# Attention layer of a two-layer graph network fed from y by feature, the first norm carried as centred weights and scales

## The chip, the cores and the metric

The kernel runs on one core of one Trainium2 chip. The metric is the device time of one execution in microseconds (us); the lower the better. Three runs of the kernel before took 954.08, 954.56 and 954.85 us, median 954.56.

## What is computed

`x` is 128 batches x 128 nodes x 128 features, `adj` a 128x128 matrix. Cut to what matters here:

```python
h = relu(einsum('ts,bsh->bth', adj, x @ Wg0 + bg0))
h = relu(einsum('ts,bsh->bth', adj, h @ Wg1 + bg1))
for p in 1..4:                     # windows of p nodes
    last = lstm_last(Wih[p-1], Whh[p-1], ..., windows of p of h)
    h[last node of each window] = last
x1 = layernorm(x + h)              # no scale, no shift, over features
Xq, Xv = x1 @ W_lin.T, x1 @ W_val.T          # 4 heads of 32
e = sum_d leaky_relu(Xq[src] + Xq[dst]) * a + log(adj[src, dst] + eps)
attn = softmax of e over the edges of one src            # 256 edges
Y = sum over edges of attn * Xv[dst], by src
out = layernorm(x1 + Y @ W_out.T)
```

## The kernel before, in words

The program has two halves, `front` and `back`, each with a function for every engine; `program` runs first the one, then the other on each engine. Nothing schedules: every engine does its instructions in the order written, and semaphores tie them together. A **tile** is 4 batches (`BT`), 512 columns; there are 32.

`front` does the two graph products and the first LSTM pass (p = 1), then `for ph in phases[1:]` the passes p = 2, 3, 4. State is kept with features on the partitions, as a pair `hT_hi` + `hT_lo`, each 128 x (128 batches x 128 nodes). An LSTM item (one step t of one group of windows) is 9 or 12 TensorE (PE) products of 512 columns from the input (L431 to L433), for t > 0 another 12 from the state (L445, L446, L449), four gate functions on ScalarE (ACT, L537) and the tanh (L525), and on VectorE (DVE) the products L762, L765, L772, L779 and the cut into hi and lo (L750, L752). The last pass, p = 4, works on 8 groups of 16 batches, two at a time ("a pair"), four steps each; the groups 6 and 7 are its last pair, and their eight items end the LSTM.

`back` goes in slots. In slot n of `for n in range(FIRST, LAST)` (n = -3 to 46) each engine works on several tiles at once:

- GpSimd (POOL): `sum_halves(n + 3)` adds hi and lo of a tile into `hsum` (L919). `factors(n)` (L940 to L958) makes the scale `rstd` and the shift of the norms from the statistics, ten small instructions, for the first norm of tile n + 2 and the second norm of tile n - 2 - LAG.
- PE: `turn_h` (L978) transposes hsum. DVE adds the residual x (`residual`, L1178) into `y` and takes statistics (`stats_in`, L1185). ACT writes the normalized tile (`normalize_x1`, L1119, four instructions with scale and bias) into `x1_kept`. PE turns that back (`turn_x1`, L985), ACT copies it out (`x1_turned`, L1145, into `x1T`), and only then `project` (L993) multiplies it with the query and value weights.
- The queries are cut into hi and lo (`query_hi` ACT L1106, `query_lo` DVE L1190), `gather` (L1002, L1003) adds them over both ends of each edge, ACT takes the leaky relu (L1141), `edge_scores` (L1012) sums with `a`. The values are cut likewise (L1110, L1195).
- Eight tiles (`GT`) make a group of the softmax, spread over four slots on DVE (`softmax`, steps 0 to 7, two a slot; step 6 is one reciprocal of 256 columns, L1220).
- LAG = GT + 4 = 12 slots later the tile's values are gathered (`value_gather`, L1037, L1038), weighted (`weight_values`, DVE L1231), summed by source (`sum_by_source`, L1054), copied (L1137), multiplied with W_out (`output`, L1065), added to x1 (`add_mixed`, DVE L1237), normalized (`stats_out` L1243, `normalize_out` ACT L1131 and POOL L925), and stored by SyncE's queue (SP).

So slots 0 to 11 hold the first half of a tile's work alone, slots 12 to 31 both halves, slots 32 to 46 the second alone. The x tiles for the residual are loaded by SP in `run_sync`, 256 KB each, two ahead.

Of the kernel before, what the change touches and what calls it, by code (L numbers as in the profile page):

```python
# [12 lines left out]
P = 128  # L13
# [9 lines left out]
BT = 4  # L23


Part = namedtuple("Part", "S CREDIT phases sync gpsimd tensor scalar vector")

# [37 lines left out]
class Tables:  # L65


    def __init__(self, sb, HEADS, E):
# [13 lines left out]
        self.minus_half = sb("minus_half", [P, 2, BT])  # L82


def front(nc, sb, sem, tables, hT_hi, hT_lo, ident, adj_sb, psum, x, adj, Wg0, bg0, Wg1, bg1, Wih, Whh, bih, bhh,
# [56 lines left out]
    bias = sb("bias", [P, SKIPS * GATES])  # L142
# [33 lines left out]
             "row_edges onehots wT_psum wT_ready adj_psum adj_done eps_done log_done diag_done log_psum log_ready ends_ready sames shifted caps")  # L176
# [14 lines left out]
    def has(k):  # L191
        return 0 <= k < tiles

# [72 lines left out]
    def run_tensor(pe):  # L266
# [43 lines left out]
        def turn_back_weights():  # L310
            pe.wait_ge(raw_loaded[1], 48)
            pe.wait_ge(S["adj_done"], EC)
# [104 lines left out]
        for ph in phases[1:]:  # L417
            for it in range(ph.iters):
# [37 lines left out]
    def run_scalar(act):  # L456
# [63 lines left out]
        for ph in phases[1:]:  # L520
            for it in range(ph.iters):
# [31 lines left out]
    def run_vector(dve):  # L553
# [66 lines left out]
        def ends_and_sames():  # L620
# [6 lines left out]
            dve.tensor_tensor(same_b[:, 0:E - 1], sorted_row[:, 0, 1:E], sorted_row[:, 0, 0:E - 1], ALU.is_equal).then_inc(S["sames"], 1)  # L627

# [92 lines left out]
        for n in range(SLOTS):  # L721
# [3 lines left out]
            elif n == 2:  # L725
                ends_and_sames()
                adjacent()
            elif n == 3:
# [9 lines left out]
        for ph in phases[1:]:  # L738
            for it in range(ph.iters):
# [15 lines left out]
                for tile, t, k, forgets in ph.body():  # L755
# [3 lines left out]
                    c = cell[s][:, 0:ph.width]  # L759
                    if t > 0:  # L760
# [30 lines left out]
def back(nc, sb, sem, tables, before, hT_hi, hT_lo, ident, psum, x, a, src, out):  # L791
# [5 lines left out]
    B = x.shape[0]  # L797
    tiles = B // BT
# [6 lines left out]
    LAG = GT + 4  # L805
    RING = LAG + 6
    X_RING = 2
    FIRST, LAST = -3, tiles + LAG + 3
# [6 lines left out]
    x1T = sb("x1T", [P, 2, TW])  # L815
# [3 lines left out]
    rows, row_a, row_b, exps = (sb(n, [P, E]) for n in ("rows", "row_a", "row_b", "exps"))  # L819
    attn = sb("attn", [P, 2, EC, P])  # L820
    x_res = sb("x_res", [P, X_RING, BT, P])
    hsum = sb("hsum", [P, 2, TW])
    y = sb("y", [P, 2, BT, P])
# [3 lines left out]
    rstd = sb("rstd", [P, 2, 2, BT])  # L827
    shift = sb("shift", [P, 2, 2, BT])
# [513 lines left out]
```

## Time and profile before

| | |
|---|---|
| median of 3 runs | 954.56 us |
| the profiled execution, its own time | 952.53 us |
| its span | 950.7 us |
| PE busy | 891.7 us (94%) |
| DVE busy | 680.2 us (72%) |
| ACT busy | 628.5 us (66%) |
| POOL busy | 207.8 us (22%) |
| last LSTM product on PE starts | 628.91 us |
| granted TensorE clock, mean | 0.988 |

Times inside the trace count from the start of the span. PE's matmul rows overlap each other, so the pace of a group is read from the starts of its neighbours, not from the length of one. A float32 product of 128 columns is two rows of the trace. The profiled execution's own time is 1.8 us above its span, and the median of the runs 2.0 us above that.

### The profile page before, as it was taken

Reading aid. Unit: us, or ns where it says so; the run is one execution under the profiler, and the core shown is the slowest. Engines: PE = TensorE matmul, PEld = TensorE weight load, DVE = VectorE, ACT = ScalarE, POOL = GpSimd, SP = SyncE. Lnnn points to the kernel's source line nnn. Section 1 sums busy time; section 2 is a strip of 40 time slices with the busy share of each in tenths; the row PEclk is TensorE's granted clock in tenths of the full one; section 3 lists DMA queues with packets and bytes.
Section 4 is the critical chain, followed back from the end, with each engine's and each line's share of the span. In section 5 each row is a group of like instructions: output and inputs, shape, how many; then the busy total and the mean of one; then the engine's idle time right before and its main releaser. Section 6 shows DMA issues by size and latency. Waiting matters only on the chain.

```text
span 950.7 us, 15626 instructions
## 1 busy us (share of the span) xinstructions
PE 891.7 (94%) x5523; PEld 771.9 (81%) x5523; DVE 680.2 (72%) x1365; ACT 628.5 (66%) x1170; POOL 207.8 (22%) x568
## 2 busy tenths in 40 slices
PE   7999999989999999999999999958879999999895
PEld 6989988868777899999987878847657888888684
DVE  5777777777877777777777776754456786776764
ACT  2777777777777776767666666646766667666354
POOL 0000000000000000000001000026755666776665
PEclk9999999999999999999999999989999999999998
DMA  4212211000000000000000000001111122221112
GB/s 117 68 46 66 59 57 52 3 23 1 0 1 1 1 1 1 1 1 2 1 1 0 1 1 1 1 22 34 50 40 35 57 68 60 58 63 36 54 57 67
DMA packets 56700, 28.67 MB, mean 30 GB/s; under 512 B 2704, under 2 KB 56624, under 8 KB 56624
## 3 DMA queue, kind: packets, MB, share of 16 engines
q1 hardware_dynamic: 55248, 27.47, 10.3%
q8 instruction: 45, 0.74, 0.3%
q10 hardware_dynamic: 1376, 0.22, 0.1%
q14 instruction: 31, 0.25, 0.1%
HBM read 19.29 MB, written 8.39 MB: 29 GB/s over the span
## 4 chain that ended last, share of the span: by engine, by line
PE 78%; DVE 7%; ACT 7%; POOL 4%; issue 3%; DVEq 0%; POOLq 0%; ACTq 0%
PE psum L431 8%; PE psum L432 8%; PE psum L433 7%; PE psum L993 6%; PE psum L449 6%; PE psum L445 6%; PE psum L446 6%; PE psum L1054 4%; PE psum L349 3%; PE psum L367 3%; PE psum L377 3%; PE psum L1065 2%; ACT x_kept L1119 2%; PE psum L341 2%; PE psum L339 2%
## 5 line engine op out<-in xcount | busy, mean ns | idle before, releaser
L537 ACT ACTIVATE work<-psum,bias 128x512 f32<-128x512 f32 (+1 forms) x408 | 234.0, 622 | 30.5 <-PE psum L449 29.9
L919 POOL TENSOR_TENSOR hsum<-hT_hi,hT_lo 128x512 f32<-128x512 f32 x32 | 41.7, 1305 | 514.7 <-DVE hT_lo L752 514.7
L431 PE MATMUL psum<-hT_hi,w_hi 128*128 128x512 f32 (+1 forms) x408 | 148.0, 363 | 2.9 <-ACT work L537 2.2
L432 PE MATMUL psum<-hT_lo,w_hi 128*128 128x512 f32 (+1 forms) x408 | 147.8, 362 | 0.0
L433 PE MATMUL psum<-hT_hi,w_lo 128*128 128x512 f32 (+1 forms) x408 | 146.7, 359 | 0.0
L525 ACT ACTIVATE work<-work 128x512 f32<-128x512 f32 (+1 forms) x112 | 63.8, 569 | 102.9 <-DVE work L772 69.3
L445 PE MATMUL psum<-hs_hi,w_hi 128*128 128x512 f32 (+1 forms) x288 | 104.0, 361 | 2.0 <-DVE hs_hi L750 1.8
L779 DVE TENSOR_TENSOR work<-work 128x512 f32<-128x512 f32 (+1 forms) x112 | 68.5, 612 | 52.0 <-ACT work L525 52.0
L449 PE MATMUL psum<-hs_lo,w_hi 128*128 128x512 f32 (+1 forms) x288 | 104.2, 362 | 0.0
L446 PE MATMUL psum<-hs_hi,w_lo 128*128 128x512 f32 (+1 forms) x288 | 103.2, 358 | 0.0
L431 PEld LDWEIGHTS psum<-hT_hi,w_hi 128*128 128x128 f32 x408 | 76.8, 188 | 16.8 <-ACT work L537 5.3
L433 PEld LDWEIGHTS psum<-hT_hi,w_lo 128*128 128x128 f32 x408 | 76.9, 189 | 10.5
L432 PEld LDWEIGHTS psum<-hT_lo,w_hi 128*128 128x128 f32 x408 | 76.7, 188 | 9.7
L765 DVE TENSOR_TENSOR work<-work 128x512 f32<-128x512 f32 (+1 forms) x112 | 69.3, 619 | 20.8 <-ACT work L537 20.8
L480 ACT ACTIVATE work<-psum,bias 128x512 f32<-128x512 f32 x96 | 64.9, 682 | 26.2 <-PE psum L341 24.1
L993 PE MATMUL psum<-w_qv,x1T 128*128 128x128 f32 x512 | 66.4, 285 | 3.0 <-ACT x1T L1145 3.0
L993 PEld LDWEIGHTS psum<-w_qv,x1T 128*128 128x128 f32 x512 | 62.4, 199 | 5.9 <-ACT x1T L1145 5.9
L1231 DVE TENSOR_TENSOR va<-psum,attn 128x512 f32<-128x512 f32 x64 | 42.8, 682 | 32.2 <-PE psum L1038 32.1
L1054 PE MATMUL psum<-from_node,va 128*128 128x128 f32 x512 | 63.2, 277 | 2.0 <-DVE x_kept L1237 2.0
L1119 ACT ACTIVATE x_kept<-y,shift,rstd 128x128 f32<-128x128 f32 x128 | 52.7, 482 | 16.0 <-POOL shift L958 16.0
L445 PEld LDWEIGHTS psum<-hs_hi,w_hi 128*128 128x128 f32 x288 | 54.1, 188 | 11.3 <-DVE hs_hi L750 4.6
L449 PEld LDWEIGHTS psum<-hs_lo,w_hi 128*128 128x128 f32 x288 | 54.1, 188 | 10.6 <-DVE hs_lo L752 4.1
(186 smaller groups left out, 1910.5 us busy)
## 6 DMA issues: line engine op xcount, KB each, us to landing
work<-x SPq DMA_DIRECT2D x32, 256.0 KB, 2.9
x_res<-x SPq DMA_DIRECT2D x32, 256.0 KB, 2.8
out<-x_kept SPq DMA_DIRECT2D x32, 256.0 KB, 2.3
work<-L_gnn_Wih SPq DMA_DIRECT2D x4, 256.0 KB, 3.1
work<-L_gnn_Whh SPq DMA_DIRECT2D x3, 256.0 KB, 2.8
bg_all<-L_gnn_bg ACTq DMA_DIRECT2D x2, 64.0 KB, 5.1
edge_row_i<-L_gnn_src SPq DMA_DIRECT2D x1, 128.0 KB, 5.6
adj_sb<-adj SPq DMA_DIRECT2D x1, 64.0 KB, 3.1
```

Of the source, the lines that this page charges most:

```text
L431: pe.matmul(out, w_hi[:, w, g, :], xh, start=True, stop=False)
L432: pe.matmul(out, w_hi[:, w, g, :], xl, start=False, stop=False)
L433: mm = pe.matmul(out, w_lo[:, w, g, :], xh, start=False, stop=(t == 0))
L445: pe.matmul(out, w_hi[:, w, g, :], hh, start=False, stop=False)
L446: pe.matmul(out, w_lo[:, w, g, :], hh, start=False, stop=False)
L449: pe.matmul(out, w_hi[:, w, g, :], hl, start=False, stop=True).then_inc(gate_psum[g], 1)
L537: op = act.activation(gate[s][g][:, 0:ph.width], psum[:, 4 * s + g, 0:ph.width], ACT.Tanh if g == G else ACT.Sigmoid, bias=bias[:, b:b + 1])
L765: op = dve.tensor_tensor(i_g, gate[s][I][:, 0:ph.width], gate[s][G][:, 0:ph.width], ALU.mult)
L779: dve.tensor_tensor(h_full[s][:, 0:ph.width], gate[s][O][:, 0:ph.width], tanh_c[s][:, 0:ph.width], ALU.mult).then_inc(S["h_mul"], 1)
L993: mm = pe.matmul(psum[:, bank, b * P:(b + 1) * P], x1T[:, k % 2, b * P:(b + 1) * P], w, start=True, stop=True)
L1054: mm = pe.matmul(psum[:, sum_bank(k), b * P:(b + 1) * P], va[:, k % 2, c, b * P:(b + 1) * P], from_node[:, c, :], start=(c == 0), stop=(c ...
L1119: op = act.activation(x1_kept[:, k % RING, b, :], y[:, k % 2, b, :], ACT.Identity, bias=shift[:, at, 0, b:b + 1], scale=rstd[:, at, 0, b:b ...
```

## The change

What it does, part by part:

1. **y by feature.** The kernel gets one more input, x with the features first, 1 MB for each of 8 groups of 16 batches. SP loads it into `x_stage`. POOL issues, for each group j, a DMA that adds `hT_hi` into `hT_lo` in place (`sum_halves(j)`), and when that has landed one that adds `x_stage` in place (`add_x(j)`); after that `hT_lo` holds y = x + h with features on the partitions. Groups 0 to 5 are done in this way one after the other, with a wait for each landing, while the LSTM runs, and only then does POOL start with `factors`. Groups 6 and 7 are spread over slots 1, 3, 5, 7 and 9, each step after that slot's `factors`, with a wait for the landing of the step before.
2. **First norm as weights and scales.** The rows of W_lin and W_val have their mean taken off in `front` (`centre_back_weights`, four DVE instructions), so `project` can take y itself as it stands in `hT_lo`; the mean needs no subtracting. The scale `rstd` goes onto the queries as they leave PSUM (`query_hi` by DVE for tiles under LAG, in four ACT instructions after; `query_lo` as four DVE instructions), onto the attention weights (`edge_rstd`, `attention_out`, now on DVE, with two more small products on PE for each group of 8 tiles), and onto x1 in `add_mixed` (four DVE instructions in place of one). Gone are `sum_halves` on POOL's arithmetic, `residual`, `normalize_x1`, `turn_x1`, `x1_turned`, and three of the ten instructions of `factors` for the first norm. New is `read_turned` on ACT, a copy of the turned y.
3. **Entry into the last LSTM pair.** The turning, reading and statistics of tiles 0 and 1 and the queries of tile 0 stand among the items of the last pair on PE, ACT and DVE. The slots run from 0 to 47.
4. LAG is 13, `RING` 24, there are 8 store semaphores, and the softmax of a group goes over five slots with its reciprocal in two halves.

```diff
+        def centre_back_weights():
+            dve.wait_ge(raw_loaded[1], 48)
+            dve.wait_ge(S["adj_done"], EC)
+            for j in range(2):
+                dve.tensor_scalar(less[:, j * P:(j + 1) * P], w_raw[1][:, j, :], -1.0 / P, 0.0, ALU.mult, ALU.add,
+                                  accum_out=minus_mean[:, j:j + 1]).then_inc(S["w_means"], 1)
+            for j in range(2):
+                dve.wait_ge(S["w_means"], j + 1)
+                dve.tensor_scalar(w_raw[1][:, j, :], w_raw[1][:, j, :], minus_mean[:, j:j + 1], None, ALU.add).then_inc(S["w_centred"], 1)
...
                 for tile, t, k, forgets in ph.body():
+                    ending = in_last_pair(ph, it, k)
+                    if ending and t == 1:
+                        entry.turned(pe, k % 2)
                     from_input(tile, t, k)
+                    if ending and t == 0:
+                        entry.turn(pe, k % 2)
+                    if is_last(ph, it, k):
+                        pe.wait_ge(S["gates_read"], ph.items_after - 1 + CREDIT)
+                        entry.query(pe)
                     if t > 0:
                         from_state(k, forgets)
...
+                    if in_last_pair(ph, it, k) and t == 0:
+                        entry.read(act, s)
...
+                    if in_last_pair(ph, it, k):
+                        if t == 1:
+                            entry.stats(dve, s)
+                        elif is_last(ph, it, k):
+                            entry.scale_query(dve)
...
-    LAG = GT + 4
-    RING = LAG + 6
-    X_RING = 2
-    FIRST, LAST = -3, tiles + LAG + 3
+    LAG = GT + 5
+    RING = LAG + 11
+    GROUP = before.phases[-1].batches // BT
+    LAST = tiles + LAG + 3
...
+        for j in range(tiles // GROUP):
+            if j:
+                sp.wait_ge(S["y_made"], 16 * j)
+            sp.dma_start(x_stage[:, :].bitcast(F32), xt[j]).then_inc(S["x_staged"], 16)
...
-            pool.tensor_tensor(hsum[:, k % 2], hT_hi[:, cols].bitcast(F32), hT_lo[:, cols].bitcast(F32), ALU.add).then_inc(S["hsum_ready"], 1)
+        def sum_halves(j):
+            cols = slice(j * GROUP * TW, (j + 1) * GROUP * TW)
+            pool.wait_ge(FS["tiles_done"], last_pass.tiles_before + j + 1 + before.CREDIT)
+            pool.dma_start(y_by_feature[:, cols], hT_hi[:, cols].bitcast(F32), accum_op=ALU.add).then_inc(S["h_summed"], 16)
+
+        def add_x(j):
+            cols = slice(j * GROUP * TW, (j + 1) * GROUP * TW)
+            pool.wait_ge(S["h_summed"], 16 * (j + 1))
+            pool.wait_ge(S["x_staged"], 16 * (j + 1))
+            pool.dma_start(y_by_feature[:, cols], x_stage[:, :].bitcast(F32), accum_op=ALU.add).then_inc(S["y_made"], 16)
...
+        sums = tiles // GROUP
+        for j in range(sums - 2):
+            sum_halves(j)
+            add_x(j)
+            pool.wait_ge(S["y_made"], 16 * (j + 1))
+        factors(-2)
+        factors(-1)
+        for n in range(LAST):
             if has(n - 3 - LAG) and not late(n - 3 - LAG):
                 normalize_out(n, n - 3 - LAG)
-            if has(n + 3):
-                sum_halves(n + 3)
             if has(n + 2) or has(n - 2 - LAG):
                 factors(n)
+            for j in (sums - 2, sums - 1):
+                at = 1 + 4 * (j - sums + 2)
+                if n == at:
+                    sum_halves(j)
+                elif n == at + 2:
+                    add_x(j)
+                elif n == at + 4:
+                    pool.wait_ge(S["y_made"], 16 * (j + 1))
...
-            pe.wait_ge(S["xT_ready"], k + 1)
             if k:
                 pe.wait_ge(free, k)
             for b in range(BT):
-                mm = pe.matmul(psum[:, bank, b * P:(b + 1) * P], x1T[:, k % 2, b * P:(b + 1) * P], w, start=True, stop=True)
+                mm = pe.matmul(psum[:, bank, b * P:(b + 1) * P], y_of(k, b), w, start=True, stop=True)
...
+        def query_hi(k):
+            dve.wait_ge(S["factors_done"], k + 1)
+            dve.wait_ge(S["q_psum"], k + 1)
+            dve.tensor_tensor(xq_hi[:, :, :], by_bank(Q), rstd[:, k, 0, :].unsqueeze(2).broadcast_to([P, BT, P]), ALU.mult).then_inc(S["q_hi"], 1)
...
         def add_mixed(m):
             dve.wait_ge(S["o_psum"], m + 1)
-            dve.tensor_tensor(x1_kept[:, m % RING], by_bank(out_bank(m)), x1_kept[:, m % RING], ALU.add).then_inc(S["o_read"], 1)
+            for b in range(BT):
+                op = dve.scalar_tensor_tensor(out=x1_kept[:, m % RING, b, :], in0=x1_kept[:, m % RING, b, :], scalar=scale_of(m, b),
+                                              in1=psum[:, out_bank(m), b * P:(b + 1) * P], op0=ALU.mult, op1=ALU.add)
+            op.then_inc(S["o_read"], 1)
```

How the order of the instructions stands at three places. First PE at the end of the LSTM, before: the last products of the last item (L445, L446, L449), then turns of tiles 0 and 1 (L978, of hsum), the second turn of tile 0 (L985), and its queries and values (L993).

```order
L449 MATMUL psum<-hs_lo,w_hi 128x512
L978 MATMUL psum<-ident,hsum 128x128 [waits f_onehots,f_a_loaded,f_ends_ready,b_hsum_ready,f_wT_ready,f_gates_read]
L978 MATMUL psum<-ident,hsum 128x128 [waits b_y_done,b_hsum_ready]
L985 MATMUL psum<-ident,x_kept 128x128 [waits b_x1_done,b_y_done]
L993 MATMUL psum<-w_qv,x1T 128x128 [waits b_xT_ready]
L993 MATMUL psum<-w_qv,x1T 128x128 x3
```

Now the same place in the change: L443 to L445 are the input products of the last item, L1058 the queries (first) and the values of tile 0, L1051 a turn of y, L1075 and L1076 the gather.

```order
L445 MATMUL psum<-hT_hi,w_lo 128x512
L1058 MATMUL psum<-w_qv,hT_lo 128x128 [waits f_wT_ready,f_gates_read]
L1058 MATMUL psum<-w_qv,hT_lo 128x128 x3
L457 MATMUL psum<-hs_hi,w_hi 128x512 [waits f_h_hi]
L458 MATMUL psum<-hs_hi,w_lo 128x512
...
L461 MATMUL psum<-hs_lo,w_hi 128x512
L1058 MATMUL psum<-w_qv,hT_lo 128x128 [waits f_a_loaded,f_onehots,f_ends_ready]
L1058 MATMUL psum<-w_qv,hT_lo 128x128 x3
L1051 MATMUL psum<-ident,hT_lo 128x128 [waits b_y_done,b_y_made]
L1051 MATMUL psum<-ident,hT_lo 128x128 x3
L1075 MATMUL psum<-ends,xq_hi 128x256 [waits f_gates_read,b_xq_ready]
```

The queries of tile 0 have moved in front of the last item's state products, the second turn is gone, and what follows the LSTM's last product is the values of tile 0, a turn, and the gather.

Second, DVE around the last LSTM item in the change (L801 to L818 are the item's products, L784 and L786 its cut): L1269 and L1279 scale the queries of tile 0, L1286 cuts its values, L1263 takes statistics of tile 2.

```order
L1269 TENSOR_TENSOR xq_hi<-psum,rstd 128x512 [waits b_q_psum,b_factors_done]
L1279 SCALAR_TENSOR_TENSOR xq_lo<-psum,rstd,xq_hi 128x128 [waits b_q_hi]
L1279 SCALAR_TENSOR_TENSOR xq_lo<-psum,rstd,xq_hi 128x128 x3
L801 TENSOR_TENSOR work<-work 128x512 [waits f_f_ready]
L804 TENSOR_TENSOR work<-work 128x512 [waits f_ig_ready]
L811 TENSOR_TENSOR work<-work 128x512 [waits f_ig_done,f_fc_done]
...
L786 TENSOR_TENSOR hT_lo<-work,hT_hi 128x128x4 [waits f_h_hi]
L1286 TENSOR_TENSOR hT_lo<-psum,hT_hi 128x512 [waits b_v_hi,f_caps,f_log_ready]
L1263 BN_STATS stats<-x_kept 128x6 [waits b_factors_done,b_y_done]
```

In the kernel before the item's first product (L762) followed the item before it directly; now the scaling of the queries, which waits for POOL's `factors_done`, stands between them.

Third, POOL in the change: the last two adding DMAs of the part ahead of the slots and the first factors (L995 to L1009, seven instructions), and further on, after the factors of slot 1, the sum for group 6.

```order
L970 DMA hT_lo<-hT_hi 128x2048
L976 DMA hT_lo<-x_stage 128x2048
L995 TENSOR_TENSOR diff<-stats 128x4
L998 TENSOR_TENSOR m_sum<-stats 128x4
L1000 TENSOR_SCALAR half_diff<-diff 128x4
L1003 TENSOR_SCALAR m_eps<-m_sum 128x4
L1005 TENSOR_TENSOR diff_sq<-half_diff 128x4
L1007 TENSOR_TENSOR var_eps<-m_eps,diff_sq 128x4
L1009 TENSOR_TENSOR rstd<-var_eps,minus_half 128x4
...
L970 DMA hT_lo<-hT_hi 128x2048
```

No `factors` stand on POOL before the twelve adding DMAs of groups 0 to 5.

## Rows read from the trace of the kernel before

**Rows 1.** Stages: us, busy PE, PEld, DVE, ACT, POOL (x), clock, DMA share, GB/s.
```profile
634.00:642.00 8.00, 1.92 (x8) 1.28 (x8) 2.76 (x10) 2.15 (x5) 5.83 (x20) 0.56 0.22 66
642.00:707.00 65.00, 53.25 (x424) 43.90 (x424) 32.80 (x76) 46.79 (x98) 42.33 (x113) 0.98 0.14 41
725.00:875.00 150.00, 148.18 (x1225) 130.88 (x1226) 109.10 (x259) 103.40 (x218) 100.08 (x239) 1.00 0.20 57
```

**Rows 2.** Chain of waits (start, us, what): starts of slots 1, 4, 5, 13.
```profile
649.25 2.07 PE psum L993 x16
...
666.32 2.06 PE psum L993 x16
...
669.00 1.55 ACT x_kept L1119 x4
...
672.01 2.06 PE psum L993 x16
...
725.08 2.05 PE psum L993 x16
```

**Rows 3.** PE timeline (start, us, line, count): the LSTM's last product.
```profile
628.91 0.39 PE L449 MATMUL psum<-hs_lo,w_hi 128*128 128x512 f32 x1
```

**Rows 4.** DVE timeline: group 4 cut; last item's first product; its cut.
```profile
593.56 0.69 DVE L752 TENSOR_TENSOR hT_lo<-work,hT_hi 128x512 fp32r<-128x512 f32 x1
...
628.00 0.69 DVE L762 TENSOR_TENSOR work<-work 128x512 f32<-128x512 f32 x1 [1.35 <-ACT work L537]
...
633.03 0.69 DVE L752 TENSOR_TENSOR hT_lo<-work,hT_hi 128x512 fp32r<-128x512 f32 x1
```

**Rows 5.** PE timeline, a slot with both halves, until the next one.
```profile
807.43 1.05 PE L1065 MATMUL psum<-w_outT,yT 128*128 128x128 f32 x8
808.32 1.95 PE L993 MATMUL psum<-w_qv,x1T 128*128 128x128 f32 x16
810.10 1.95 PE L1054 MATMUL psum<-from_node,va 128*128 128x128 f32 x16
811.98 0.64 PE L1012 MATMUL psum<-leaky,a_wide 128*32 128x256 f32 x8
812.55 0.50 PE L1037 MATMUL psum<-hT_hi,to_r 128*128 128x512 f32 x1
...
813.13 0.64 PE L978 MATMUL psum<-ident,hsum 128*128 128x128 f32 x4
...
814.71 0.62 PE L985 MATMUL psum<-ident,x_kept 128*128 128x128 f32 x4
815.09 0.36 PE L1002 MATMUL psum<-ends,xq_hi 128*128 128x256 f32 x1
...
816.54 1.95 PE L993 MATMUL psum<-w_qv,x1T 128*128 128x128 f32 x16
```

**Rows 6.** DVE timeline of that slot: four statistics, and the instruction after.
```profile
809.24 0.87 DVE L1243 BATCH_NORM_STATS2 stats<-x_kept 128x6 f32<-128x128 f32 x4
810.04 0.69 DVE L1190 TENSOR_TENSOR xq_lo<-psum,xq_hi 128x512 fp32r<-128x512 f32 x1
```

**Rows 7.** POOL timeline: first and last of the ten of `factors`.
```profile
635.31 0.20 POOL L940 TENSOR_TENSOR diff<-stats 128x4 f32<-128x4 f32 x1 [115.05 <-DVE stats L1185]
...
638.35 0.20 POOL L958 TENSOR_TENSOR shift<-minus_mean,rstd 128x4 f32<-128x4 f32 x1
```

**Rows 8.** Chain of waits: slot 32's first sum, one turn of the late slots.
```profile
883.76 2.02 PE psum L1054 x16
...
923.56 1.17 PE psum L1065 x8
...
931.87 1.17 PE psum L1065 x8
```

**Rows 9.** DMA queue of SP (packets, MB, share of 16 engines' span).
```profile
q1 hardware_dynamic: 55248, 27.47, 10.3%
```

**Rows 10.** DMA issues: x tiles (KB each, us from issue to landing).
```profile
x_res<-x SPq DMA_DIRECT2D x32, 256.0 KB, 2.8
```

More of the change, by code:

```diff
@@ L26 @@
 Part = namedtuple("Part", "S CREDIT phases sync gpsimd tensor scalar vector")
+Entry = namedtuple("Entry", "turn turned query read stats scale_query")
 class LstmPhase:
@@ L1080, in slot @@
             if has(n + 2):
-                turn_h(n + 2)
+                turn(n + 2)
             if has(n):
@@ L1246, in slot @@
         def slot(n):
+            if n > 0 and n % GT == LAG % GT and has(n - LAG):
+                attention_out((n - LAG) // GT)
             if has(n - 2 - LAG):
@@ L1250, in slot @@
             if has(n):
-                query_lo(n)
+                if n:
+                    scaled_query(n)
                 value_lo(n)
-            g, quarter = softmax_at(n)
-            if g is not None:
-                softmax(g, 2 * quarter)
+            g, part = softmax_at(n)
+            for step in STEPS[part][0] if part is not None else ():
+                softmax(g, step)
             if has(n - LAG):
@@ L1258, in slot, with enter_stats, enter_scale_query, run_vector @@
             if has(n + 2):
-                residual(n + 2)
-                stats_in(n, n + 2)
+                stats_in(n + 2)
             if has(n - LAG):
                 weight_values(n - LAG, 1)
-            if g is not None:
-                softmax(g, 2 * quarter + 1)
+            for step in STEPS[part][1] if part is not None else ():
+                softmax(g, step)
+        return stats_in, scaled_query, slot
+    def enter_stats(dve, k):
+        stats_in, _, _ = vector_steps(dve)
+        stats_in(k)
+    def enter_scale_query(dve):
+        _, scaled_query, _ = vector_steps(dve)
+        scaled_query(0)
+    def run_vector(dve):
+        _, _, slot = vector_steps(dve)
         dve.wait_ge(FS["log_ready"], 1)
         dve.wait_ge(FS["caps"], 2)
-        for n in range(FIRST, LAST):
+        for n in range(LAST):
             slot(n)
-    return Part(S, 0, None, run_sync, run_gpsimd, run_tensor, run_scalar, run_vector)
-def program(nc, x, adj, Wg0, bg0, Wg1, bg1, Wih, Whh, bih, bhh, W_lin, W_val, a, W_out, src, dst, out):
+    entry = Entry(enter_turn, enter_turned, enter_query, enter_read, enter_stats, enter_scale_query)
+    return Part(S, 0, None, run_sync, run_gpsimd, run_tensor, run_scalar, run_vector), entry
+def program(nc, x, xt, adj, Wg0, bg0, Wg1, bg1, Wih, Whh, bih, bhh, W_lin, W_val, a, W_out, src, dst, out):
     B = x.shape[0]
@@ L1301, in _ @@
                 second.sync(sp)
+            @block.tensor
+            def _(pe):
+                first.tensor(pe, entry)
+                second.tensor(pe)
+            @block.scalar
+            def _(act):
+                first.scalar(act, entry)
+                second.scalar(act)
+            @block.vector
+            def _(dve):
+                first.vector(dve, entry)
+                second.vector(dve)
             @block.gpsimd
```

288 lines of the change are left out of this document (152 added, 136 removed).

## The prediction

> **What bounds the kernel now.** I read the busy times by stage first, then the chain of waits, then one slot of each stage on the engines that meet there. The stages differ. While the LSTM runs, PE has no gap; its last product starts at 628.91 [rows 3], so it ends about 629.1. Then comes a hole: from 634 to 642 PE is busy 1.92 of 8 us and its granted clock is down to 0.56, half of full speed [rows 1]: the first tile goes through addition, statistics, factors, normalization and a second turn before a projection can start, and slot 1 starts only at 649.25 [rows 2]. In the early slots PE is busy 53 of 65 us [rows 1] but the chain runs through ACT: projection, the cut of the values, four normalizing instructions (1.55 us), the second turn, its copy, next projection. A slot takes 672.01 - 666.32 = 5.69 us [rows 2]. Slots 1 to 12 take 725.08 - 649.25 = 75.8 us, 7.5 above twelve times 5.69; those are the slots in which DVE's softmax and the first gathers begin. In the slots with both halves PE is full (148.2 of 150 us [rows 1]) and one takes 816.54 - 808.32 = 8.22 us [rows 5]. The late slots hang on a loop (output, add, statistics, factors, normalization, copy, output) that covers two slots in 931.87 - 923.56 = 8.31 us [rows 8].
>
> **The sum**, along the path, against the profiled execution (span 950.7).
>
> *Front.* Four DVE instructions of 128 columns and their waits; a DVE instruction of that size is spaced 0.2 us in rows 6, so about 1 us with the waits, and PE waits for `w_centred` before three transposes. PE has other work queued only behind them. I take +0.5, bounds 0 and 1.5.
>
> *Last pair.* PE is full, so what is put in counts whole. Turning y reads hT_lo with a step of four elements, as the turns of hsum do. Sixteen rows show 1.95 us and eight 1.05, so a row is (1.95 - 1.05)/8 = 0.112 apart from the next and the last one lasts 0.26; four strided turns show 0.64, so 0.12 to 0.127 each [rows 5]. I take 0.12; the four contiguous turns (0.62) leave it open that the step costs nothing. Eight turns and eight rows of queries: +1.9. ACT's two copies of a turned tile and DVE's statistics stand where PE has its t = 0 and t = 1 products queued; cover gone, the statistics alone would cost 1.6. So PE ends its last product at 631.5, DVE its last cut at 633.03 + 0.69 + 2.4 = 636.1 [rows 4].
>
> *Entry.* DVE then cuts the values of tile 0 (0.7, as L1190 in rows 6), takes statistics (0.8, the spacing in rows 6), scales and cuts the queries of tile 1. Four DVE instructions of 128 columns that read PSUM have no row: from below four statistics, 0.80 [rows 6]; from above the four of ACT, 1.55 [rows 2]; I take 0.95, near the row of the same engine. So 636.1 + 0.7 + 0.8 + 0.8 + 0.95 = 639.3, and the gather of slot 1 starts there. On PE it lies 1.8 + 0.6 + 0.5 behind the slot's start, so slot 1 counts from 636.4 instead of 649.25. **-12.9.** Nothing is idle for long, so the clock should not fall to half.
>
> *Early slots.* ACT's normalization leaves the loop. What is late next is PE: 8.22 less the sum by source (811.98 - 810.10 = 1.88), output (0.89), two value gathers (0.58 each), the second turn (815.09 - 814.71 = 0.38), all from rows 5, is 3.93; with the projection now loading with a step of four, 16 rows at 0.12 instead of 0.112, +0.12: 4.05. DVE needs 0.7 + 0.95 + 0.7 + 0.8 = 3.15. POOL's ten instructions take 638.35 + 0.20 - 635.31 = 3.24 us [rows 7]; three of them go, one of which hung on a wait of its own, so 2.6. Factors made in slot n are used in slot n + 2 and end about 7.2 us after slot n starts; they are wanted at 9.2, 2 us later. Twelve slots: 48.6, and of the 7.5 us of softmax and first gathers I keep 5.5, since the reciprocal is halved but DVE now scales the queries too (bounds 0 and 12). Slot 13 starts at 636.4 + 54.1 = 690.5 instead of 725.08. **-21.7** more.
>
> *Slots with both halves.* Minus the second turn, plus the strided loads: 8.22 - 0.38 + 0.12 = 7.96. DVE has 109.1 of 150 us now, 6.0 a slot [rows 1]; it loses the residual (0.6) and gains twice 0.3, so it stays under 6.5. Before, 19 slots took 883.76 - 725.08 = 158.7 [rows 2, 8]. Now 158.7 - 19 x 0.26 = 153.8, less 1.9 for the sum by source that slot 13 has not yet (the lag is one more), plus 0.3 for the small products of each of three groups: 152.8. **-5.9.** Slot 32 at 843.3.
>
> *Late slots.* Before, 950.7 - 883.76 = 66.9. One slot more, 4.15, and in each of the 16 half of the 0.3 by which four instructions in `add_mixed` exceed one: +2.4. 73.5. **+6.6.** End at 916.8.
>
> *The adding DMAs.* No row shows one. Let D be the time from POOL's issue to the landing. From below: a copy. SP's queue moved 27.47 MB in 10.3% of 950.7 us of all engines [rows 9], 3.57 us a MB, so 3.7 for one transfer; a 256 KB load lands after 2.8 us [rows 10], 1.9 more than its own 0.9. That gives 5.6. An addition reads two operands: 1.9 + 7.4 = 9.3 if reads set the pace. I take **8**, between them, since rows of 8 KB replace packets of half a KB and SP's loads of x share the engines. From above I keep reads and writes each at half that speed, 1.9 + 14.8 = 16.7; nothing in the trace excludes it. Twice D matters. First, group 4 is cut at 594.2 [rows 4], then four additions and the first factors (2.7) must pass before DVE may scale the queries, wanted at about 629.1 (the last item's first DVE product is at 628.00 [rows 4]). The stall is 594.2 + 4D + 2.7 - 629.1 = 4D - 32.2, and it stands in front of the last LSTM item, whose products, cuts and all slots queue behind it. Second, the sum for group 6 is issued behind the factors of slot 1, at about 636.4 + 7.2 = 643.6. Each wait holds the factors behind it: four times D and another 2.6 must have passed when the factors of slot 10 are wanted in slot 12, at about 636.4 + 44.6 + 3.7 + 1.1 = 685.8. That stall is 4D - 39.6. At 8 both are nothing. POOL's issue costs about 1 us in a slack of 2.
>
> The Trainium skill, "Collectives: The Full Stack", in its section on why ReduceScatter is half of AllGather, says that an adding transfer runs at half the pace of a copy because it reads two sources; "DMA: Bandwidth & Descriptors", Anatomy of one DMA, gives 2.0 us plus the bytes by 436 GB/s for a copy. By these an addition would take an estimated 6.8 us and the sum would not change, since both stalls are nothing there too; the trace of before has no accumulating transfer to agree or disagree.
>
> *SP's queue*: the stores now stand behind all loads of x. The last load waits for group 6, in about slot 5; the first store is in slot 16. Nothing.
>
> Sum: 950.7 - 12.9 (the 2.4 of front and last pair are in it) - 21.7 - 5.9 + 6.6 = 916.8 span, 918.6 as that execution's own time (952.53 against 950.7), 2.0 more for the median (954.56): **920.6**.
>
> **Rivals.**
> *A, as summed*, 909 to 932 by the bounds of the softmax extra (-5.5, +6.5), the reads, and the four-piece instructions. Chance 0.52.
> *B, additions a little slow*, D from 9 to 13. At 11: 11.8 + 4.4 = 16.2 more, 937. For it: two reads already give 9.3. Against it: that row is of small packets. 0.17.
> *C, another engine's order binds the slots.* DVE has 15 instructions a slot in fixed order, each waiting for PE, ACT or POOL; if the early slots take 5 us instead of 4.05 (+11) and the full slots stay at 8.22 (+5), 936. For it: before, early slots were bound by exactly such a chain with PE at 82%. Against it: the four-instruction link is gone and every remaining one has slack. 0.18.
> *D, slower than before: the additions hold the LSTM's last item.* At D = 16.7 the stalls are 34.6 and 27.2, 982. It decides from 8D - 71.8 = 34, D = 13.2. In front of the last pair only 35 us are free, and POOL does nothing else for it. Chance 0.11.
> *E*, that y is not there in time for other reasons and the gain is eaten to no change: 0.02.
> That the change does not do what it says: the second turn and the normalization are gone from the order, so the gain in PE's products is certain; only its cover can fail, which is C.
>
> A measurement of this kernel tells about 0.2% from no change. Faster A, B and C, 0.87; same 0.02; slower 0.11. The range takes A, C and most of B: 906 to 948; what it leaves out is D, the end of B, and a gain beyond 48 us.
>
> **What would show it.** Right: PE without a gap over 1 us between the last LSTM product and slot 2, clock at 1.00; early slots of 4.0 to 4.3 us; projection rows 0.12 apart; full slots at 8.0; late loop 8.6 for two slots; landing of the additions at 8 us. Wrong: DVE idle before the scaling of tile 0's queries with POOL as releaser (B, D); DVE idle in slots 4 to 10 on POOL's `rstd`; early slots of 5 us with PE waiting for DVE's query cut (C).

## The result, and the profile after

| | before | after |
|---|---|---|
| median | 954.7 us (954.08 to 954.91, 4 runs) | 974.12 us (973.65 to 975.92, 4 runs) |
| span of the profiled execution | 950.7 us | 972.1 us |
| PE busy | 891.7 us (94%) | 933.5 us (96%) |

The change makes the kernel slower, by about 2%: the ratio of the times is 1.0208, 95% interval 1.019 to 1.0226, clear of no change. The forecast was 920.6 us and a range of 906 to 948. PE has 112 matmul rows fewer (5411 against 5523) and is busy 42 us longer.

The page of the kernel after, its groups of instructions for the projection, and the queue of the adding transfers (packets, MB, share):

```profile
L1058 PE MATMUL psum<-w_qv,hT_lo 128*128 128x128 f32 x512 | 124.9, 397 | 1.0 <-DVE hT_lo L1286 1.0
L1058 PEld LDWEIGHTS psum<-w_qv,hT_lo 128*128 128x128 f32 x512 | 122.1, 328 | 1.3 <-DVE hT_lo L1286 1.2
...
q0 software_dynamic: 2304, 16.78, 8.5%
```

The same groups of the kernel before, by shape, with both kinds of turn:

```profile
L993 PEld LDWEIGHTS psum<-w_qv,x1T 128*128 128x128 f32 x512 | 62.4, 199 | 5.9 <-ACT x1T L1145 5.9
L978 PEld LDWEIGHTS psum<-ident,hsum 128*128 128x128 f32 x128 | 19.4, 207 | 11.0 <-issue 8.3 <-ACT work L537 1.2
L985 PEld LDWEIGHTS psum<-ident,x_kept 128*128 128x128 f32 x128 | 13.8, 143 | 25.7 <-DVE y L1178 20.2 <-issue 5.3
```

Here is the answer. The stationary operand is the one that PE loads ahead of a product (the rows PEld), the moving operand the one that then streams through. The projection's 512 loads of a stationary operand took 199 ns each and take 328; the time in which PE is loading for it goes from 62.4 to 122.1 us. The turns show that it was to be seen: a load with a step of four (L978) took 207 ns, one of neighbouring columns (L985) 143, but the spacing of the turns hardly showed it [rows 5].

The chain of waits of the kernel after: the projections that start slots 2, 3 and 4, then slots 13 and 14, then 16 and 17, then the sum that starts slot 32.

```profile
644.45 3.73 PE psum L1058 x16
650.37 3.73 PE psum L1058 x16
656.28 3.73 PE psum L1058 x16
...
711.44 3.81 PE psum L1058 x16
718.59 3.73 PE psum L1058 x16
...
737.97 3.73 PE psum L1058 x16
747.65 3.73 PE psum L1058 x16
...
896.65 2.02 PE psum L1131 x16
```

Sixteen rows take 3.73 us, 0.233 apart, where before they were 0.112 apart [rows 5]. An early slot takes 5.91 us (5.69 before [rows 2]), a full one 9.68 (8.22 before [rows 5]).

Stages of the kernel after (same columns as [rows 1]): at the entry PE is idle for 1.0 us of 8 where it had been idle for 6.1 [rows 1], its clock does not fall, and in the full slots DVE, ACT and POOL have less to do per microsecond than before.

```profile
634.00:642.00 8.00, 6.96 (x37) 6.77 (x36) 7.76 (x19) 3.39 (x7) 2.08 (x7) 1.00 0.01 5
740.00:890.00 150.00, 149.16 (x984) 136.49 (x984) 101.23 (x310) 73.56 (x172) 69.36 (x193) 1.00 0.10 27
```

The adding transfers. POOL's timeline: group 4's and group 5's two additions each, and the first factors (the bracket is POOL's wait); then the DMA issues, KB each and us to landing:

```profile
595.87 0.87 POOL L970 DMA_DIRECT2D hT_lo<-hT_hi  x1 [9.77 <-DVE hT_lo L786]
603.67 0.86 POOL L976 DMA_DIRECT2D hT_lo<-x_stage  x1 [6.93 <-DMA hT_lo<-hT_hi]
610.92 0.86 POOL L970 DMA_DIRECT2D hT_lo<-hT_hi  x1 [6.39 <-DMA hT_lo<-x_stage]
623.02 0.88 POOL L976 DMA_DIRECT2D hT_lo<-x_stage  x1 [11.24 <-DMA hT_lo<-hT_hi]
630.10 0.20 POOL L995 TENSOR_TENSOR diff<-stats 128x4 f32<-128x4 f32 x1 [6.19 <-DMA hT_lo<-x_stage]
```

```profile
x_stage<-x_by_feature SPq DMA_DIRECT2D x8, 1024.0 KB, 5.1
hT_lo<-hT_hi POOLq DMA_DIRECT2D x8, 1024.0 KB, 8.0
hT_lo<-x_stage POOLq DMA_DIRECT2D x8, 1024.0 KB, 7.0
```

From one issue to what POOL does when it has landed, the four took 34.2 us, 8.6 each: 7.1 to 7.8 for three of them, and 12.1 for the one at 610.92, beside which SP loads the next 1024 KB of x. DVE's timeline shows what that held up, the scaling of tile 0's queries in front of the last LSTM item, and DVE's last cut:

```profile
632.77 0.69 DVE L1269 TENSOR_TENSOR xq_hi<-psum,rstd 128x512 fp32r<-128x512 f32 x1 [3.09 <-POOL rstd L1009]
...
638.78 0.69 DVE L786 TENSOR_TENSOR hT_lo<-work,hT_hi 128x512 fp32r<-128x512 f32 x1
```

### The profile page after: what moved, and what is told of

Read it like the earlier page. It is cut to its first block, busy times and chain, and to the rows that moved or that the text cites. A ratio compares the mean times of both kernels' runs of the same rounds, so it can differ in the third digit from the quotient of the medians.

```text
span 972.1 us, 15304 instructions
## 1 busy us (share of the span) xinstructions
PE 933.5 (96%) x5411; PEld 820.3 (84%) x5411; DVE 698.1 (72%) x1560; ACT 581.0 (60%) x1084; POOL 173.0 (18%) x509
## 4 chain that ended last, share of the span: by engine, by line
PE 86%; DVE 6%; ACT 3%; issue 2%; POOL 2%; DMA 1%; ACTq 0%; DVEq 0%; POOLq 0%
PE psum L1058 12%; PE psum L443 8%; PE psum L444 8%; PE psum L445 8%; PE psum L461 6%; PE psum L457 6%; PE psum L458 6%; PE psum L1131 4%; PE psum L361 3%; PE psum L379 3%; PE psum L389 2%; PE psum L1142 2%; PE psum L352 2%; PE psum L351 2%; PE psum L353 2%
## 5 line engine op out<-in xcount | busy, mean ns | idle before, releaser
L443 PE MATMUL psum<-hT_hi,w_hi 128*128 128x512 f32 (+1 forms) x408 | 148.7, 364 | 3.3 <-ACT work L559 2.6
L445 PE MATMUL psum<-hT_hi,w_lo 128*128 128x512 f32 (+1 forms) x408 | 147.2, 361 | 0.0
L1058 PE MATMUL psum<-w_qv,hT_lo 128*128 128x128 f32 x512 | 124.9, 397 | 1.0 <-DVE hT_lo L1286 1.0
L1058 PEld LDWEIGHTS psum<-w_qv,hT_lo 128*128 128x128 f32 x512 | 122.1, 328 | 1.3 <-DVE hT_lo L1286 1.2
L818 DVE TENSOR_TENSOR work<-work 128x512 f32<-128x512 f32 (+1 forms) x112 | 68.5, 612 | 54.1 <-ACT work L545 54.1
L970 POOL DMA_DIRECT2D hT_lo<-hT_hi x8 | 7.3, 918 | 556.5 <-DVE hT_lo L786 537.3
L443 PEld LDWEIGHTS psum<-hT_hi,w_hi 128*128 128x128 f32 x408 | 76.8, 188 | 17.4 <-ACT work L559 5.4
L445 PEld LDWEIGHTS psum<-hT_hi,w_lo 128*128 128x128 f32 x408 | 76.8, 188 | 10.8
L1131 PEld LDWEIGHTS psum<-from_node,va 128*128 128x128 f32 x512 | 60.0, 192 | 6.8 <-issue 4.8
```

The lines of the kernel that those rows point to most:

```text
L443: pe.matmul(out, w_hi[:, w, g, :], xh, start=True, stop=False)
L445: mm = pe.matmul(out, w_lo[:, w, g, :], xh, start=False, stop=(t == 0))
L818: dve.tensor_tensor(h_full[s][:, 0:ph.width], gate[s][O][:, 0:ph.width], tanh_c[s][:, 0:ph.width], ALU.mult).then_inc(S["h_mul"], 1)
L1058: mm = pe.matmul(psum[:, bank, b * P:(b + 1) * P], y_of(k, b), w, start=True, stop=True)
L1131: mm = pe.matmul(psum[:, sum_bank(k), b * P:(b + 1) * P], va[:, k % 2, c, b * P:(b + 1) * P], from_node[:, c, :], start=(c == 0), stop=(c ...
```

## The experiments

Two theories stood against each other. **S**: what costs is the step of four elements with which the projection now reads its stationary operand. **R**: it is something else that came along, the place of the operand in hT_lo or the transfers. All times below are medians, beside runs of the kernel before on the same chip (953.7, 954.37 and 953.93 us in the three sets).

### The step alone, taken out and put in

Neighbouring columns in the changed kernel:

```diff
-                mm = pe.matmul(psum[:, bank, b * P:(b + 1) * P], y_of(k, b), w, start=True, stop=True)
+                at = k * TW + b * P
+                mm = pe.matmul(psum[:, bank, b * P:(b + 1) * P], y_by_feature[:, at:at + P], w, start=True, stop=True)
```

> The changed kernel, but the projection reads 128 columns of hT_lo that lie next to one another, in place of every fourth one. The queries and values then belong to other nodes and batches: this part of the computation is changed, its shapes, instruction counts and waits are not; the turns keep their step of four. Theory S (the step in the stationary operand of the projection is what costs): the rows of the projection go back from 0.233 to 0.112 us apart, a slot falls from 9.69 to 7.8 and an early one from 5.91 to 4.0 to 4.4, and the median is 974 - 31 x 1.94 = 914, or up to 925 where another engine then sets the early slots. Rival R (something else that came with the change, the place of the operand in hT_lo or the addition's transfers, slows PE): the rows stay at 0.23 and the time within 5 us of 974.

Measured: 920.78 us (919.98 to 922.05), ratio to before 0.966 (0.9646 to 0.9675). S. The loads, and two early slots of its chain of waits (4.11 us a slot; a full one takes 7.75):

```profile
L1059 PEld LDWEIGHTS psum<-w_qv,hT_lo 128*128 128x128 f32 x512 | 61.2, 195 | 3.7 <-DVE hT_lo L1287 3.5
...
650.86 1.78 PE psum L1059 x16
654.97 1.79 PE psum L1059 x16
```

The step of four in the kernel before, in place of neighbouring columns:

```diff
-                mm = pe.matmul(psum[:, bank, b * P:(b + 1) * P], x1T[:, k % 2, b * P:(b + 1) * P], w, start=True, stop=True)
+                mm = pe.matmul(psum[:, bank, b * P:(b + 1) * P], x1T[:, k % 2, :].rearrange("p (t b) -> p b t", b=BT)[:, b, :], w, start=True, stop=True)
```

> The kernel before with one edit: its projection reads x1T with a step of four elements, as the changed one reads hT_lo. The order of nodes in queries and values is changed, so that part of the computation is. Theory S: the projection's rows go from 0.112 to 0.23 apart in SBUF memory of another tensor as well, 1.94 us more in each of the 19 slots in which PE is full and in the early ones, where the projection is a link of the chain: 954.7 + 31 x 1.94 = 1015, bounds 995 (late slots and some early ones hide it) and 1020. Rival R (it is hT_lo or the transfers, not the step): 955.

Measured: 1010.24 us (1009.63 to 1010.47), ratio 1.0596 (1.0581 to 1.0612), 56 us on a kernel that has none of the rest of the change. Two slots of its chain of waits, early (slots 3 and 4) and full:

```profile
666.23 4.01 PE psum L993 x16
673.85 4.01 PE psum L993 x16
...
839.47 3.73 PE psum L993 x16
849.62 3.73 PE psum L993 x16
```

7.62 and 10.15 us a slot against 5.69 and 8.22 [rows 2, 5]: 1.93 more in both kinds, as S has it. R falls on both sides.

### How the price goes with the step

The same edit as the first, with a step of two and of three:

```diff
+                at = k * TW + b // 2 * 2 * P + b % 2
+                mm = pe.matmul(psum[:, bank, b * P:(b + 1) * P], y_by_feature[:, at:at + 2 * P - 1:2], w, start=True, stop=True)
```

```diff
+                at = k * TW + b
+                mm = pe.matmul(psum[:, bank, b * P:(b + 1) * P], y_by_feature[:, at:at + 3 * P - 2:3], w, start=True, stop=True)
```

> The changed kernel with the projection's stationary operand read with a step of two elements (8 bytes) instead of four (16 bytes); queries and values belong to other nodes and batches, that part is changed. Rule L (the read is cut into pieces of 16 bytes, and is free while two of its elements lie in each): rows 0.112 to 0.12 apart, time as in the run with neighbouring columns, about 916. Rule P (the price grows with the step): rows about 0.15 to 0.17 apart, 3.73 us for the 16 become 2.4 to 2.8, time 935 to 945. Rule N (any step costs the same): 0.23, 974.

> The changed kernel with the projection's stationary operand read with a step of three elements (12 bytes): queries and values belong to other nodes and batches, that part is changed. If a read is free while two of its elements lie in a piece of 16 bytes and costs by the piece otherwise: 128 elements lie in 96 pieces, against 64 at a step of two and 128 at a step of four; by pieces above 64 the price is half of that of step four, 16 rows in 2.75 us, 948 us. If the price is a switch that any step over two throws: 3.73 us and 974.

Measured: 923.11 us (922.75 to 924.35) with a step of two, 947.19 (946.32 to 948.56) with three. The projection's loads in the groups by shape, first with a step of two, then of three:

```profile
L1059 PEld LDWEIGHTS psum<-w_qv,hT_lo 128*128 128x128 f32 x512 | 63.9, 198 | 3.3 <-DVE hT_lo L1287 3.2
```

```profile
L1059 PEld LDWEIGHTS psum<-w_qv,hT_lo 128*128 128x128 f32 x512 | 93.0, 264 | 2.6 <-DVE hT_lo L1287 2.6
```

198, 264 and 328 ns at 8, 12 and 16 bytes: 128 elements then lie in 64, 96 and 128 pieces of 16 bytes, and above 64 each piece costs 2 ns. Below 64 there is next to nothing: neighbouring columns, 32 pieces, took 195 ns. A step of two is so nearly free, not quite: a full slot takes 7.84 us with it, 7.75 without, and the kernel 2.3 us more. The guess by pieces had been 948 us for three. No step above four was run, so these loads alone do not tell pieces of 16 bytes from bytes spanned, which grow alike up to there.

The Trainium skill, "Advanced Engine Details and Errata", SBUF Cachelines, says that SBUF is read in lines of 16 bytes and needs two hits on a line for full pace. By that rule a step of two is free and one of four is not, and these three loads agree with it, but for the 3 ns of the step of two. I had not weighed it in the forecast; it is the rule that spoke against this change.

### A repair by layout that fails elsewhere

If a step of two is as good as free, let all blocks of h lie in pairs of batches instead of fours. Nothing is left out, and the projection reads with a step of two:

```diff
+PAIR = 2
-    hi_bt = hT_hi[:, :].rearrange("p (n t b) -> p n t b", t=P, b=BT)
+    hi_bt = hT_hi[:, :].rearrange("p (n t b) -> p n t b", t=P, b=PAIR)
-        blocks = ph.batches // BT
+        blocks = ph.batches // PAIR
...
-        return y_by_feature[:, k * TW:(k + 1) * TW].rearrange("p (t b) -> p b t", b=BT)[:, b, :]
+        return y_by_feature[:, k * TW:(k + 1) * TW].rearrange("p (h t b) -> p h b t", t=P, b=PAIR)[:, b // PAIR, b % PAIR, :]
...
```

> Nothing of the computation is left out: every block of h and of x by feature is laid out in pairs of batches (node, then batch 0 or 1; then node, batch 2 or 3) instead of fours, in the GNN, the LSTM and the attention layer alike, so that y is read with a step of two elements. Theory L (a step of two is free, as the run with step two measured at 923): 921 to 925 us, under the kernel before's 953.7 by 3%. Rival M: the LSTM now reads its windows and writes its h in runs of two elements instead of four; if that slows the moving operand of its products or DVE's cuts, the LSTM's part of the time grows, and a tenth more on some 800 products of 360 ns that read windows would be 29 us, 950. I take L at 0.7.

Measured: 1143.41 us (1142.46 to 1144.76), ratio 1.198 (1.196 to 1.1999). The projection is as wished (198 ns a load), and M came true at more than seven times its 29 us. PE's timeline in the last LSTM pass: three products that read windows of h, then two that read the state, which lies in one run.

```profile
702.34 0.64 PE L444 MATMUL psum<-hT_hi,w_hi 128*128 128x512 f32 x1
702.80 0.65 PE L445 MATMUL psum<-hT_lo,w_hi 128*128 128x512 f32 x1
703.27 0.64 PE L446 MATMUL psum<-hT_hi,w_lo 128*128 128x512 f32 x1
703.73 0.42 PE L458 MATMUL psum<-hs_hi,w_hi 128*128 128x512 f32 x1
703.99 0.40 PE L459 MATMUL psum<-hs_hi,w_lo 128*128 128x512 f32 x1
```

The same place in the changed kernel, where the windows' columns come in fours:

```profile
560.01 0.38 PE L444 MATMUL psum<-hT_lo,w_hi 128*128 128x512 f32 x1
560.23 0.40 PE L445 MATMUL psum<-hT_hi,w_lo 128*128 128x512 f32 x1
560.47 0.38 PE L443 MATMUL psum<-hT_hi,w_hi 128*128 128x512 f32 x1
```

0.465 apart against 0.23: a moving operand of 512 columns in runs of two elements is read at half pace, in runs of four at the pace of the state's products beside it. Both layouts span the same 2048 elements, so here it is the pieces and not the bytes spanned. Here two elements of each piece of 16 bytes are used, and it is not free, so the rule of two hits that held for the weight load does not hold for this operand; counted in pieces, 256 at 0.465 us are 1.8 ns each, much as the loads' 2 ns. The 1224 such products of the passes 2 to 4 account for the loss: 336 of 512 columns in pass 2 at 0.22 more, 360 of 512 columns in pass 4 at 0.235 and 528 of 336 columns in pass 3 at 0.15 are 238, of which 222 showed against the run with a step of two (spans 1143.0 and 921.0).

Two more edits were tried on top of this layout: the first factors made earlier, and POOL's additions of groups 6 and 7 spread over more slots (both are shown below).

> The kernel with pairs, and POOL makes the factors of tiles 0 and 1 before it waits for group 4's second addition instead of after it. Theory H: DVE waited 3.1 us on rstd before the last LSTM item's cuts in the changed kernel, but had 1.5 us of other slack there, so 1.5 us less than the run with pairs alone, bounds 0.5 and 3.1. Rival: PE has its products queued and the cuts are late for another reason, then 0.

> The kernel with pairs and the factors first, and POOL's additions for groups 6 and 7 spread: second addition of group 6 in slot 5 (not 3), its wait in slot 9, group 7 in slots 10, 14 and 18. In the run with neighbouring columns POOL waited 2.62 us for group 6's first addition, which took 10.52 us beside another transfer, and the factors behind it made DVE's scaling wait 0.9 us. Theory W: 1 to 2 us less than the version with the factors first. Rival: the slots after it make the time up, 0.

Measured: 1142.83 and 1142.8 us, within 0.6 of 1143.41, whose own runs lie 2.3 apart. Neither shows in a kernel whose PE is busy 97% of the span, so this pair tells nothing of the two edits.

### The first factors earlier, alone

```diff
             add_x(j)
+            if j == 4:
+                factors(-2)
+                factors(-1)
             pool.wait_ge(S["y_made"], 16 * (j + 1))
-        factors(-2)
-        factors(-1)
```

> The changed kernel with one edit: POOL makes the factors of tiles 0 and 1 after it has issued group 4's second addition, not after it has waited for it and for group 5's. It prices the front stall alone. Theory H: DVE's wait of 3.09 us on rstd goes, and as about half of it delayed anything, the time falls by 1.5 us, to 972.6, bounds 971 and 973.6. Rival: 0.

Measured: 972.83 us (972.41 to 973.98), ratio 1.0198 (1.0185 to 1.0212) against 1.0208 (1.019 to 1.0226) without it. 1.3 us less by the medians and 1.5 by the spans, but the intervals overlap, and the kernel before was 0.8 faster too in the runs beside it. So a gain of about 1 us is likely but not shown. The mechanism is plain in DVE's timeline, where POOL is no longer what it waits for:

```profile
631.01 0.69 DVE L1270 TENSOR_TENSOR xq_hi<-psum,rstd 128x512 fp32r<-128x512 f32 x1 [1.76 <-PE psum L1059]
```

### Repairs by a copy

POOL copies each tile's y once, batch by batch, into a ring of three blocks (`x1_kept` gives up three), with the first factors earlier as above. In the first version turns and projection read the copy:

```diff
+        def flatten(k):
+            pool.wait_ge(S["y_made"], 16 * (k // GROUP + 1))
...
+            pool.tensor_copy(y_flat[:, k % Y_RING, :].rearrange("p (b t) -> p b t", b=BT),
+                             y_by_feature[:, k * TW:(k + 1) * TW].rearrange("p (t b) -> p b t", b=BT)).then_inc(S["y_flat"], 1)
...
                 factors(n)
+            if has(n + 3):
+                flatten(n + 3)
```

> A version meant to beat both: the changed kernel, but POOL copies each tile's y once to a ring of three blocks, one batch after the other, so that turns and projection read neighbouring columns; the ring x1_kept gives up three blocks for it; and the first two sets of factors are made before POOL waits for group 4's second addition, not after it. POOL's copy of 512 columns is taken at 1.3 us, as its addition of that size before, in slots where POOL has at least 3.5 us to spare. Theory S: rows 0.112 apart, slots of 7.7 to 8.0 and 4.0 to 4.4, 912 to 924 us, and the DVE wait of 3.09 us on rstd before the last item gone. Rival R: 965 to 974. Rival Q (POOL's added copy makes the factors late): early slots of 5 us, 930.

Measured: 941.78 us (941.3 to 942.09), ratio 0.9879 (0.9862 to 0.9895). Faster than before by 1.2%, and 18 to 30 us short of what I expected. The waits of 645 to 690 us name a ring of engines:

```profile
POOL diff L1005 <- DVE stats L1279: 15.6, 8, 2.3
DVE stats L1279 <- ACT x_kept L1227: 15.1, 8, 2.8
ACT x_kept L1227 <- PE psum L1067: 14.8, 7, 3.1
PEld psum L1067 <- POOL y_flat L985: 13.3, 7, 2.5
```

Statistics, factors, POOL's copy, turn, ACT's copy, statistics: 6 us round, since the copy stands behind the factors on POOL and the turn waits for it. Moving the copy ahead of the factors breaks the ring:

```diff
+            if has(n + 3):
+                flatten(n + 3)
             if has(n + 2) or has(n - 2 - LAG):
                 factors(n)
-            if has(n + 3):
-                flatten(n + 3)
```

> The first version (POOL's copy for turns and projection) with one edit: POOL copies tile n + 3 ahead of the factors of slot n instead of behind them. If the loop through POOL was what cost it, the early slots fall from 6.1 to 4.2 us or a little more, as the copy must then wait for the projection of the same slot (its block of the ring comes free there), and the time to 920 to 930. If POOL's added work is what costs, 938 to 942 as before.

Measured: 921.49 us (920.96 to 922.21), 20 us less. In the second version the turns read hT_lo as in the change, only the projection reads the copy, and the copy (of tile n + 2) is ahead of the factors too:

```diff
     def y_of(k, b):
-        return y_flat[:, k % Y_RING, b * P:(b + 1) * P]
+        return y_by_feature[:, k * TW:(k + 1) * TW].rearrange("p (t b) -> p b t", b=BT)[:, b, :]
...
         def turn(k):
-            pe.wait_ge(S["y_flat"], k + 1)
+            pe.wait_ge(S["y_made"], 16 * (k // GROUP + 1))
...
-                mm = pe.matmul(psum[:, bank, b * P:(b + 1) * P], y_of(k, b), w, start=True, stop=True)
+                mm = pe.matmul(psum[:, bank, b * P:(b + 1) * P], y_flat[:, k % Y_RING, b * P:(b + 1) * P], w, start=True, stop=True)
```

> A second version meant to beat both, and nothing of the computation is left out. The first one (y copied by POOL for turns and projection) measured 942: there a tile's turn, copy, statistics, factors and the next tile's POOL copy stood in one loop of 6 us. Here the turns read hT_lo with the step of four again, which costs them nothing that shows, and only the projection reads POOL's copy; POOL makes the copy of tile n + 2 in slot n ahead of the factors, while it would wait for statistics. Theory T (the loop is what cost the first version 21 us): early slots of 4.1 us and full ones of 7.8 to 8.0, 918 to 924. Rival: POOL, with 1.15 us more in each slot beside DVE, slows DVE or makes the factors late, slots of 4.8 and 8.3, 935 or more.

Measured: 920.67 us (920.39 to 921.28), ratio 0.9649 (0.9636 to 0.9662). And with the additions of groups 6 and 7 spread:

```diff
             for j in (sums - 2, sums - 1):
-                at = 1 + 4 * (j - sums + 2)
+                at = 1 + 9 * (j - sums + 2)
                 if n == at:
                     sum_halves(j)
-                elif n == at + 2:
+                elif n == at + 4:
                     add_x(j)
-                elif n == at + 4:
+                elif n == at + 8:
                     pool.wait_ge(S["y_made"], 16 * (j + 1))
```

> The version that copies for the projection alone, and POOL's additions for groups 6 and 7 spread: issued in slots 1, 5, 10 and 14 instead of 1, 3, 5 and 7, waited for in 9 and 18 instead of 5 and 9. Theory W: the wait behind a 10.5 us addition in slot 3 goes, 1 to 2 us less than without it. Rival: 0, as the two versions with pairs showed (1142.8 both, though PE had no gap there to save).

Measured: **918.71 us** (918.55 to 918.94), ratio 0.9628 (0.9615 to 0.9641), 2.0 less than without it. It beats the kernel before by 35 us and the changed one by 55, with the whole computation in it. Its chain of waits, slots 2 to 4 and 15 to 17:

```profile
642.94 1.78 PE psum L1074 x16
647.05 1.78 PE psum L1074 x16
651.18 1.78 PE psum L1074 x16
...
705.39 1.79 PE psum L1074 x16
713.14 1.79 PE psum L1074 x16
720.89 1.79 PE psum L1074 x16
```

4.11 and 7.75 us a slot; the forecast for the change itself had 4.05 and 7.96.

## Why the prediction was wrong

**The failed step** is the price of the strided read in "Early slots" and "Slots with both halves": "with the projection now loading with a step of four, 16 rows at 0.12 instead of 0.112, +0.12". It is 16 rows at 0.233, +1.94 (3.73 against 1.79). In 31 slots that is 31 x (1.94 - 0.12) = 56.4 us, as much as the 55.3 by which the span was missed; taken out, it gave back 53.3 (974.12 to 920.78). I took the price from the four strided turns [rows 5], where 0.12 was the spacing of rows of which each has a weight load of 207 ns beside it, and carried it to the projection, where the load with the same step takes 328. The spacing of the turns only says that 207 ns fit beside the other rows. The trace held both loads' lengths (207 strided, 143 not) and I read neither; that alone would have asked for an upper bound. The words "the four contiguous turns (0.62) leave it open that the step costs nothing" bounded the step from below and never from above.

By the steps, against the profiled execution (forecast 916.8, span 972.1):

| stage | forecast | after | off by |
|---|---|---|---|
| start of slot 2 | 636.4 + 4.05 = 640.45 | 644.45 | +4.0 |
| slots 2 to 12 | 50.05 | 711.44 - 644.45 = 67.0 | +16.9 |
| slots 13 to 31 | 152.8 | 896.65 - 711.44 = 185.2 | +32.4 |
| slot 32 to the end | 73.5 | 75.5 | +2.0 |

*Slots 2 to 12*: 11 x (5.91 - 4.05) = +20.5, less 3.5 because softmax and first gathers cost 2.0 and not 5.5 (67.0 - 11 x 5.91). *Slots 13 to 31*: 19 x (9.68 - 7.96) = +32.7. Without the step a full slot takes 7.75, where the forecast without its 0.12 has 7.84, so the rest of that sum was 0.09 too high; an early slot takes 4.11 where it has 3.93, 0.18 too low.

**What held.** With the step taken out, the changed kernel runs at 920.78 us, where 920.6 was forecast. That this is so close is partly luck, and the parts say by how much (its chain: slot 2 at 646.52, slot 32's sum at 844.9, span 920.2): +6.1, -4.5 for the slots up to 31, +1.8. Rival C, the engines' order, does not bind: 4.11 us a slot. The gain in PE's products was real, as was the cover for it.

**The additions.** D was forecast as 8. In the changed kernel and in the one with neighbouring columns it is 7.0 to 8.4, but 10.5 to 12.1 where a load of x starts with it, and 8.6 in the mean of the four that count first, for which the formula 4D - 32.2 gives a stall of 2.0; DVE waited 3.09. Rival D (additions hold the last LSTM item, decides at D = 13.2) is the mechanism of that wait, but not the cause: taking the wait away gave 1.3 us or less, of the 53.5 by which the median was missed. The kernel came out slower for a reason that was none of my rivals.

**Entry.** The last cut came at 638.78 + 0.69 = 639.5, not 636.1. POOL's late factors make 1.4 of it (with them early, the next instruction, the cut of tile 0's values, starts at 637.99 in place of 639.39); of the other 2 us, 0.8 is the step again, as DVE then waits for the eight strided rows of tile 0's queries, which take 1.74 us and not 0.96; the last 1.2 I have not taken apart. The best version still starts slot 2 at 642.94, 2.5 over the forecast. In the **late slots** the four pieces of `add_mixed` take 1.12 us, where 0.95 was forecast; 16 uses of which half lies on the path make 1.4 of the 2.0.

## What to carry to other kernels

Before a matrix product reads its stationary or moving operand with a step, count the 16-byte pieces of each row that it touches: here 128 float32 were loaded at nearly full pace from up to 64 pieces, each further one cost 2 ns, and a moving operand wanted runs of four. A strided read that costs nothing in a transpose is no evidence for a product; take the length of the weight load, not the spacing of its rows, in a view that keeps the operands apart. Where a layout suits one reader and costs another, one copy by an engine with time to spare was worth 52 us here (972.83 to 920.67), with the copy outside the ring of waits; inside it, 31 (972.83 to 941.78).

## What the runs showed of the hardware beyond that

*The price depends on what the load feeds.* The same step of four adds 64 ns to the load of a turn (207 against 143) and 129 ns to that of a float32 product (328 against 199). I had expected one price for the read. Why it is twice as much for the product no run here tells.

*With the load mended, the clock fell.* With neighbouring columns and the factors late, PE sat idle for 3.35 us before tile 1's values; its timeline, and the stage after it (columns as [rows 1]):

```profile
640.67 2.08 PE L1059 MATMUL psum<-w_qv,hT_lo 128*128 128x128 f32 x8 [3.35 <-DVE hT_lo L1287]
```

```profile
640.00:646.00 6.00, 5.33 (x27) 4.30 (x28) 4.32 (x15) 1.49 (x3) 2.21 (x7) 0.50 0.01 3
```

The granted clock is 0.50, that is 1.2 instead of 2.4 GHz, and eight rows take 2.08 us. With a step of two PE was idle for 3.00 us there, in the first copying version with the copy ahead for 2.85, and in both the clock of this stage was 0.72. In the last version, with the factors early, PE waited 1.97 us there and the clock stayed at 1.00:

```profile
640.00:646.00 6.00, 5.94 (x53) 4.62 (x52) 5.13 (x16) 2.88 (x5) 5.21 (x15) 1.00 0.01 3
```

Slot 2 starts 3.6 us earlier in it (642.94 against 646.52), of which no run tells the clock's part from that of the shorter wait. In the changed kernel itself PE, with its slow loads, waited only 1.04 us there, and the clock stayed at 1.00. *Adding transfers* of 1024 KB from SBUF to SBUF took 7.0 and 8.0 us in the median, and 10.5 to 12.1 beside a load of the same size.
